# Attention with its adjacency term: where the term is added, and the order of the last iteration

## What is computed

```python
scale = DIM_HEAD ** (-0.5)
q, k, v = ...
dots = einsum('bhid,bhjd->bhij', q, k) * scale
m2 = mask[:, None, :, None] & mask[:, None, None, :]
dots = where(m2, dots, -big)
attn = softmax(dots, axis=-1) * 0.33
adj = where(m2, adj[:, None], 0.0)
dist = where(m2, adj[:, None], big)
attn = attn + 0.33 * adj + 0.33 * exp(-dist)
out = einsum('bhij,bhjd->bhid', attn, v)
out = out.reshape(B, N, 512) @ W_out + b_out
```

## Time and profile before

| | |
|---|---|
| median of 3 runs | 2669.83 us (2668.64 to 2670.15) |
| the profiled execution | 2667.08 us |
| its span, from first to last instruction | 2665.1 us |
| mean granted clock of TensorE | 0.999 |
| TensorE busy | 2590.1 us, 97% |
| VectorE busy | 1856.3 us, 70% |
| ScalarE busy | 893.6 us, 34% |
| GpSimd busy | 469.0 us, 18% |
| HBM traffic | 36 GB/s over the span |

### The profile page before, as it was taken

How to read it: one execution, slowest core, us unless ns; L and a number is a source line. 1 busy time by engine, 2 the same in 40 slices (tenths; PEclk the granted TensorE clock), 3 DMA queues, 4 the chain that set the end, 5 groups by cost and what they waited for, 6 DMA issues and landing times.

```text
span 2665.1 us, 74512 instructions
## 1 busy us (share of the span) xinstructions
PE 2590.1 (97%) x30297; PEld 2183.5 (82%) x30297; DVE 1856.3 (70%) x4168; ACT 893.6 (34%) x2796; POOL 469.0 (18%) x746
## 2 busy tenths in 40 slices
PE   7999999999999999999999999999999999999998
PEld 5788888887888888788888888888888888888887
DVE  5888888888888888866655665764665665566565
ACT  3222222222222222343432432433333243243333
POOL 1222222222222222210110111011011011101101
PEclk9999999999999999999999999999999999999999
DMA  3211111111111111311101101101110110110100
GB/s 129 83 39 39 39 40 39 39 39 39 39 39 39 39 39 39 115 32 35 36 15 31 35 19 29 35 19 32 35 31 16 35 35 15 31 35 19 29 20 17
DMA packets 128229, 100.87 MB, mean 38 GB/s; under 512 B 86676, under 2 KB 88744, under 8 KB 127912
## 3 DMA queue, kind: packets, MB, share of 16 engines
q1 hardware_dynamic: 125872, 95.18, 11.6%
q10 hardware_dynamic: 2040, 1.13, 0.1%
HBM read 62.68 MB, written 33.55 MB: 36 GB/s over the span
## 4 chain that ended last, share of the span: by engine, by line
PE 86%; DVE 7%; ACT 3%; issue 2%; POOL 2%; DMA 0%; ACTq 0%; DVEq 0%; POOLq 0%
PE ps L1317 23%; PE ps L631 18%; PE ps L1302 14%; PE ps L1320 11%; PE ps L634 9%; PE ps L623 4%; PE ps L1344 3%; PE ps L1382 1%; PE ps L1357 1%; PE ps L1389 1%; POOL sm L261 1%; DVE sm L480 1%; POOL sm L263 1%; DVE sm L478 1%; ACT Fp L351 1%
## 5 line engine op out<-in xcount | busy, mean ns | idle before, releaser
L1174 DVE TENSOR_TENSOR Tl<-ps,Th 128x256 fp32r<-128x256 f32 (+1 forms) x576 | 227.7, 446 | 88.9 <-ACT Th L1100 74.7
L987 POOL TENSOR_TENSOR Fp<-Fp,mhalf 128x1 f32<-128x1 f32 x128 | 78.6, 614 | 1175.2 <-DVE Fp L1181 1175.2
L631 PE MATMUL ps<-W1h,Th 128*128 128x512 f32 x512 | 205.9, 402 | 1.9 <-DVE Tl L453 1.8
L631 PE MATMUL ps<-W2h,Th 128*128 128x512 f32 x512 | 203.9, 398 | 3.1 <-DVE Tl L488 1.1
L631 PE MATMUL ps<-W1l,Th 128*128 128x512 f32 x512 | 200.8, 392 | 0.0
L631 PE MATMUL ps<-W2l,Th 128*128 128x512 f32 x512 | 199.9, 390 | 0.0
L1105 ACT ACTIVATE R<-R 128x512 f32<-128x512 f32 x128 | 80.9, 632 | 352.2 <-DVE R L1215 352.2
L1129 ACT ACTIVATE E<-E,Fp 128x64 f32<-128x64 f32 x512 | 170.8, 340 | 32.5 <-DVE Fp L1249 31.3
L261 POOL TENSOR_SCALAR sm<-sm 128x1 f32<-128x1 f32 x192 | 78.9, 411 | 557.8 <-DVE sm L482 298.9
L1241 DVE COPY QK<-ps 128x512 f32<-128x512 f32 x64 | 44.1, 689 | 166.7 <-PE ps L1302 166.7
L1302 PE MATMUL ps<-Th,Wh 128*128 128x256 f32 x512 | 147.7, 288 | 0.0
(11 more groups left out here) (208 smaller groups left out, 6657.2 us busy)
## 6 DMA issues: line engine op xcount, KB each, us to landing
X<-in_x SPq DMA_DIRECT2D x64, 256.0 KB, 6.3
x<-R SPq DMA_DIRECT2D x64, 256.0 KB, 2.4
X<-x SPq DMA_DIRECT2D x64, 256.0 KB, 2.7
out<-E SPq DMA_DIRECT2D x64, 256.0 KB, 2.1
AB<-in_adj SPq DMA_DIRECT2D x504, 8.0 KB, 1.7
NX<-in_adj SPq DMA_DIRECT2D x128, 32.0 KB, 2.2
E<-in_L_W1T SPq DMA_DIRECT2D x8, 256.0 KB, 6.8
E<-in_L_W SPq DMA_DIRECT2D x4, 512.0 KB, 5.1
```

The costliest lines, as they stand in the source:

```text
L631: pe.matmul(out, Th[:, c, j * P:(j + 1) * P], R(j), start=(j == 0 and R is Rh), stop=False)
L1174: return dve.tensor_tensor(lo, ps, hi.bitcast(F32), ALU.subtract)
```

## The change

Four things are changed.

1. The adjacency term is built from the turned adjacency `AT` instead of the separately loaded `A`. Per tile it is 128x64 (rows j of the graph, columns i), so for four tiles 128x256 where `Cm` was 128x512. The eight loads of `A` are gone; two loads of a mask row in another layout (`mrowT`) and one of a mask column are new. On POOL the masks are multiplied first (the new `MT` before `MM`), the bias `BS` is next, and then come `BT`, the sum and its masking, all of them now 128x256. The exponential on ACT and `BT` on POOL now wait for both turnings (at_ok), and the turning of the next group (at) waits for both of them.
2. sm no longer adds the term. After ta has turned the attention in PSUM, one VectorE instruction (L1272 of the changed kernel) reads all 128x512 of it, adds `CT` and writes `AA`. ScalarE's part of ta is gone. TensorE signals once behind all four transposes, and av waits for that one instruction.
3. `END` is a list of its own, and `TRANSITION` is another list. `ORDER` is as it was.
4. SP's loop over the iterations of the second half is written out instead of looping on the engine. The vectors gamma, beta and a are loaded at the start of the program into the tile `Fp`, which is not yet used there, instead of an own tile.

```diff
-        A, MM, BT = (per_graph(W) for W in (flat(first.NX), first.v_all[:, :], first.wa_all[:, :]))
-        Cm, BS = (per_graph(first.adjacent[:, k:k + 2, :, :].rearrange("p a c j -> p (a c j)")) for k in (0, 2))
+        MM, BS = (per_graph(W) for W in (first.v_all[:, :], first.adjacent[:, 2:4, :, :].rearrange("p a c j -> p (a c j)")))
+        MT, BT = (first.wa_all[:, k * CH * C:(k + 1) * CH * C].rearrange("p (c i) -> p c i", c=CH) for k in range(2))
+        CT = first.adjacent[:, 0, :, :]
...
+        END = order(
+            "sm.0 sm.1 qk.1 ta.0 ta.1 rs4.0 s.2 av.0 av.1 s.3 sm.2 wo.0 z4.0 wo.1 sm.3 ta.2 ta.3 rs4.1 x4.0 av.2 wo.2 z4.1 "
+            "bo.2 x4.1 rs4.2 bo.3 av.3 wo.3 rs4.3 z4.2 z4.3 x4.2 x4.3")
...
# POOL, step cm
-                pool.tensor_scalar(BT[:, :, :, :], A[:, :, :, :], LG, None, ALU.mult).then_inc(bt3, 1)
+                pool.tensor_tensor(MT[:, :, :], MT[:, :, :], mcf[:, 2, :].unsqueeze(2).to_broadcast([P, CH, C]), ALU.mult)
...
+                for p in range(2):
+                    pool.wait_ge(at_ok[p], n)
+                pool.tensor_scalar(BT[:, :, :], AT[:, :, :], LG, None, ALU.mult).then_inc(bt3, 1)
...
-                pool.tensor_tensor(Cm[:, :, :, :], Cm[:, :, :, :], BT[:, :, :, :], ALU.add).then_inc(cm2, 1)
+                pool.tensor_tensor(CT[:, :, :], CT[:, :, :], BT[:, :, :], ALU.add).then_inc(cm2, 1)
                 pool.wait_ge(cm2, n)
-                pool.tensor_tensor(Cm[:, :, :, :], Cm[:, :, :, :], MM[:, :, :, :], ALU.mult).then_inc(cm_ok, 1)
+                pool.tensor_tensor(CT[:, :, :], CT[:, :, :], MT[:, :, :], ALU.mult).then_inc(cm_ok, 1)
...
# ACT, step cm
+                        act.copy(MT[:, :, :], mrowT[:, :, :])
                         act.copy(MM[:, :, :, :], mrow[:, :, :, :]).then_inc(row_ok, 1)
-                        act.activation(Cm[:, :, :, :], A[:, :, :, :], ACT.Exp, bias=ln_ld[:, :], scale=-1.0).then_inc(exp_adj, 1)
+                        for p in range(2):
+                            act.wait_ge(at_ok[p], each[ahead])
+                        act.activation(CT[:, :, :], AT[:, :, :], ACT.Exp, bias=ln_ld[:, :], scale=-1.0).then_inc(exp_adj, 1)
...
-                    if step == "ta":
-                        act.wait_ge(ta_psA, n[c])
-                        act.copy(AV(c)[:, 0:2 * P], psA[c][:, 0:2 * P]).then_inc(ta_sbA, 1)
...
# DVE, step at
+                        if each[ahead] > 1:
+                            dve.wait_ge(exp_adj, each[ahead] - 1)
+                            dve.wait_ge(bt3, each[ahead] - 1)
...
# DVE, steps sm and ta
-                            .then_inc(soft_ok, 1)
-                        dve.wait_ge(soft_ok, 3 * n[c])
+                            .then_inc(attn_ok, 1)
+                    if step == "ta":
+                        dve.wait_ge(ta_ps, n[c])
                         dve.wait_ge(cm_ok, each[ahead])
-                        dve.tensor_tensor(E4(c), E4(c), over_heads(Cm, c), ALU.add).then_inc(attn_ok, 1)
-                    if step == "ta":
-                        dve.wait_ge(ta_psB, n[c])
-                        dve.tensor_copy(AV(c)[:, 2 * P:4 * P], psB[c][:, 0:2 * P]).then_inc(ta_sbB, 1)
+                        dve.tensor_tensor(AV(c).rearrange("p (x m i) -> p x m i", x=2, i=C), scores(c).rearrange("p x n (y i) -> p x (n y) i", y=2),
+                                          CT[:, c, :].unsqueeze(1).unsqueeze(1).to_broadcast([P, 2, 4, C]), ALU.add).then_inc(ta_sb, 1)
...
# PE, steps ta and av
-                        for x, ready in enumerate((ta_psA, ta_psB)):
+                        for x in range(2):
...
-                            mm.then_inc(ready, 1)
+                        mm.then_inc(ta_ps, 1)
...
-                        alone(ta_sbA, n[c])
-                        pe.wait_ge(ta_sbB, n[c])
+                        alone(ta_sb, n[c])
```

More of the change, by code:

```diff
@@ L856, in convolutions_and_attention @@
             "xp.2+ x3.3+ qk.0+ xp.3+ cm.0+ v.2+ v.3+ s.0+ bo.1+ s.1+")
-        START, END = [e for e in ORDER if e[2]], [e for e in ORDER if not e[2]]
+        END = order(
+            "sm.0 sm.1 qk.1 ta.0 ta.1 rs4.0 s.2 av.0 av.1 s.3 sm.2 wo.0 z4.0 wo.1 sm.3 ta.2 ta.3 rs4.1 x4.0 av.2 wo.2 z4.1 "
+            "bo.2 x4.1 rs4.2 bo.3 av.3 wo.3 rs4.3 z4.2 z4.3 x4.2 x4.3")
         def pair_counts(it, reg):
             return [[reg(it * 2 + (a * 2 + p + 1)) for p in range(2)] for a in (0, 1)]
-        MASK_LOADS = 2 * CH + 1 + 4
+        MASK_LOADS = 1 + 4 + 2 + 1
         TRANSITION = [(int(half), entry) for half, entry in ((e[0], order(e[2:])) for e in (
[8 rows of a table removed]
-            "2:s.1+").split())]
[7 rows of a table added]
+            "2:bo.0+ 2:xp.2+ 2:z3.3+ 2:g2.3+ 2:x3.3+ 2:qk.0+ 2:rs3.3+ 2:xp.3+ 2:v.2+ 2:bo.1+ 2:cm.0+ 2:v.3+ 2:s.0+ 2:s.1+").split())]
         block = ctx.enter_context(nc.Block())
@@ L890, in load_masks @@
             def load_masks(tile):
[L892 to L895, removed]
                 sp.dma_start(mrow[:, :, :, :], mask_rows[bass.ds(tile, CH)].rearrange("t (g j) -> (t g j)", g=2).partition_broadcast(P))\
@@ L901, in load_masks @@
                                      allow_slow_non_contiguous=True).then_inc(masks_in, 16)
+                for g in range(2):
+                    sp.dma_start(mrowT[g * C:(g + 1) * C, :, :], mask_halves[g, bass.ds(tile, CH), :].partition_broadcast(C))\
+                        .then_inc(masks_in, 16)
+                sp.dma_start(mcol[:, 2, :], mask_cols[:, bass.ds(tile, CH)], allow_slow_non_contiguous=True).then_inc(masks_in, 16)
             def load_qkv(k):
@@ L948, in store @@
                 sp.dma_start(out_rows[bass.ds(t0 + c, 1)].rearrange("a r d -> (a r) d"), Z[c % 2]).then_inc(out_stored[c % 2], 16)
-            with sp.Fori(0, iters - 1) as it:
-                t0 = sp.snap(it * CH)
+            for it in range(iters - 1):
+                t0 = it * CH
                 for p in range(2):
                     for c in (2 * p, 2 * p + 1):
-                        sp.wait_ge(t_ps[0], sp.snap(t0 + (c + 1)))
-                        sp.wait_ge(b3_ok, sp.snap(t0 + (c + 1)))
+                        sp.wait_ge(t_ps[0], t0 + (c + 1))
+                        sp.wait_ge(b3_ok, t0 + (c + 1))
                         load_x(c, t0 + (CH + c))
-                    sp.wait_ge(at_ok[p], sp.snap(it + 1))
+                    sp.wait_ge(at_ok[p], it + 1)
                     load_blocks(t0 + CH, p)
-                sp.wait_ge(cm_ok, sp.snap(it + 1))
+                sp.wait_ge(cm_ok, it + 1)
                 load_masks(t0 + CH)
@@ L1108, in steps @@
                         if each[ahead] > 1:
-                            act.wait_ge(attn_ok, (each[ahead] - 1) * CH)
+                            act.wait_ge(ta_sb, (each[ahead] - 1) * CH)
                         else:
```

23 lines of the change are left out of this document (13 added, 10 removed), and 15 rows, old and new, of the table TRANSITION.

## The result

| | before | after |
|---|---|---|
| median | 2668.89 us (5 runs, 2667.95 to 2670.15) | 2656.32 us (5 runs, 2654.58 to 2659.42) |
| ratio | | 0.9953, 95% interval 0.9939 to 0.9968 |
| profiled execution, span | 2667.08, 2665.1 | 2656.32, 2654.1 |
| mean granted clock | 0.999 | 0.999 |

Faster by 12.6 us where 7.6 were forecast, just outside the range. The sign and the end are as forecast, the hand-over has the wrong sign, and the loop gained almost three times its term.

A forecast was written before the change was run, and what follows sets the result against it. TensorE, busy 97%, was taken as the bound, so only its waits and clock pay. Loop -3.3, hand-over -0.3, end -2.4, clock -1.6 sum to -7.6 us: 2662.2 us from a median of 2669.83, range 2656.5 to 2668.5.

The forecast's parts named there:

- Place one: Before the first output projection wo.0 in each loop turn: VectorE's whole evictions make wo.0 0.14 us later.
- (c): Rival: slower, VectorE's eviction becomes the bound, +9 us in the loop less 2.4, 2676.4 us; chance 0.07.
- Places two and three: Before t0.0 and g0.0 in each turn: without the SBUF add g0.0 comes 0.22 us earlier, wo.0's delay included.
- The loop term: 15 turns of the attention loop, each 0.22 us shorter: -3.3 us.
- Everything at zero: ScalarE, GpSimd and the DMA queue: their changed work counted as zero, covered while TensorE works on projections.
- Hand-over: Between the halves, new list: y3.1 fills a 2.56 us wait, y3.2 loses cover; -0.3 us, between -1.5 and +1.
- The weight piece: In the hand-over's new list: a weight piece is moved ahead into a pause; part of the -0.3 us term.
- The end: Last iteration: wo.3 starts earlier, -2.4 us, and the clock stays up there, -1.6 us.
- The clock term: Last projection wo.3: the clock stays up instead of falling to half, -1.6 us, the less sure term; other end 0.
- (a): Rival: the gain stays at the end alone, the loop gives 0; 2665.8 to 2667.4 us; chance 0.31.
- (b): Rival: the loop gains but the clock falls all the same at the end; 2663.8 us; chance 0.14.
- (d): Rival: no wait follows g0.0's chain, -0.5 us a turn, -7.5 for the loop; 2658.0 us; chance 0.06.

The follow-up runs named there:

- b1: Changed kernel with the old TRANSITION, the old END and 32 spare bytes in front of Vh; 2663.41 us, ratio to before 0.9977.
- d3: Kernel before with 32 spare bytes in front of Vh, the new END and y3.1 alone moved ahead, without the moved term; 2663.56 us against 2670.27.
- a1: Kernel before with 32 unused bytes in front of the value weights Vh and Vl; 2666.35 us against 2670.21, ratio 0.9985.
- c3: Changed kernel with the old TRANSITION, in which only y3.1 is moved, in front of t3.2; its hand-over took 160.17 us.
- c4: Changed kernel with its new TRANSITION, in which only y3.1 is moved back behind t3.2; its hand-over took 161.71 us.
- a4: Changed kernel with the old END, the last iteration following the rest of ORDER; 2658.73 us.
- a2: Changed kernel with 32 spare bytes in front of Vh and Vl; 2660.99 us.
- c1: Changed kernel with the old TRANSITION, 32 spare bytes in front of Wh and 96 behind Wl; 2677.79 us against 2669.24 before.
- d1: Changed kernel with the old TRANSITION, y3.1 alone ahead of t3.2, 32 spare bytes in front of Wh and 224 behind Wl; 2652.50 us, ratio 0.9936.
- d2: c3 run again: changed kernel with the old TRANSITION and y3.1 alone in front of t3.2; 2655.98 us against 2670.27 before.
- a3: Changed kernel with the old TRANSITION; 2656.95 us against 2670.21 before.

## Why the prediction was wrong

It forecast a gain of 7.6 us; 12.6 were measured. Against its steps:

- **Place one**: +0.14 us at wo.0; measured +0.10. The step with two starts 0.61 apart holds (1.20 for two). The evicting add takes 0.69 us, as the sum assumed; by the Trainium skill's figures (VectorE: DVE Perf Modes, the section on the TRN2 errata) it would have been, as an estimate, 65 ns dearer, and the trace doesn't show that. Nor did the eviction by one engine become a bound, which was rival (c): VectorE's busy time fell from 1856 to 1829 us.
- **Places two and three**: g0.0 0.22 earlier with the 0.14 included; measured 0.30, and 0.32 (b1) and 0.34 (d3) a turn in the experiments. The chain was read right but 0.08 too long: t0.0 came 0.31 earlier, not 0.25, and from x4.0 to the remainder were 0.45 us, not 0.5. The chain then ended before TensorE did, so what bounds g0.0 now is av.2 behind its new wait of 0.25 us. The loop term should have been -4.5, not -3.3: under-sized, mechanism right.
- **Everything at zero**: the step that failed. The prediction counted engines and queues and has no term for where the tiles lie. The new mask tiles move Vh from 224 to 0 modulo 256 bytes against the features: 48 matmuls a turn by 5.8 ns, 0.28 us, 15 times, is -4.2. The trace before had a sign of it: around v.1 the eight matmuls of W2h stand 0.229 us apart, the twelve of the values 0.234. Without a run that moves the tile (a1) nothing said that the place was the reason.
- **Hand-over**: -0.3 forecast, +2.0 measured, beyond the bound of +1. y3.1 in front of the wait does no harm (c3), but its gain of 0.3 is not shown either. The weight piece "moved ahead into a pause" was mis-read: the pause is ScalarE's, but VectorE's part of the piece runs beside an operation of GpSimd for gs.3 and makes it 0.83 us longer, t2.3 waits 0.65 longer, and the rest of the list costs 1.35 us in all (c4). What of the last 0.4 is the turning's was not taken apart. The rest of the 2.0, some 0.6, is the clock, which fell in this profiled execution and not in that of before. It is no property of the new list: it fell in 3 of the 5 profiled executions with the old list, 4 of the 7 with the new one, and in none of the 4 with y3.1 alone ahead, which are too few to show a rule. The prediction had taken the clock into account only at the end.
- **The end**: -4.0 forecast, -4.0 measured. wo.2 came 8.88 us behind wo.0 (forecast 8.98), wo.3 13.61 (forecast 13.48), the clock stayed up. Of this 1.4 us need the term in the eviction (d3), which the prediction counted under the list. The clock term is no property of the old END: with it the clock fell in a4 and not in b1, which is worth 1.5 us.
- **The chances**: rivals (a) and (c) are out, and so is (b), since the clock stayed up before wo.3; (d), no wait behind g0.0's chain, is half true: no wait is left there, but it gives 0.30 a turn and not 0.5. Without the shifted weights (a2) the change measures 9.2 us, inside the range.

The sum as it should have stood: -4.5 - 4.2 + 2.0 - 4.0 = -10.7 of the 11.0 between the spans. The rest is +0.6 in the first half and -0.8 in the loop, where three turns of before were up to 0.5 us longer than the others. In two of them t0.0 waits 0.69 us instead of 0.34, in the third av stops for 0.36; why stays open.

## What to carry to other kernels

Adding a term in an eviction that must happen anyway is worth the removed operation only as far as a wait stands behind it: read the three or four waits that its queue feeds, and what comes next in each. A change that adds or drops a tile moves all that is allocated behind it: compare the start addresses of both operands of the hot matmuls, modulo 256 bytes, before and after. And a list with several moves should be tried one move at a time, and a pause looked for on every engine that the moved step uses: here one move did no harm, and the others together cost 1.35 us.

## What the runs showed of the hardware

- Matmuls of 128x512 in fp32r follow each other by 0.2275 us when the tiles of moving and stationary operand start 0 apart modulo 256 bytes (0.2299 for the values in c1), and by 0.2333 at 32, 160, 192 and 224, a little less at 128. In c1, where all six weights other than the values are away from 0, it was 21 us of 2656, the gain in the queries and keys included. What in the chip makes the distance count is not shown.
- With stationary weights and moving features of 256 columns the sign turns: 0.1208 us at distance 0, 0.1184 to 0.1188 at 32 (d1), 160, 192 and 224. A third of them read their stationary operand from Th and Tl themselves, where the low halves of these weights lie, so their distance never changes; from d2 to d1 they speed up like the others (119.8 and 120.0 ns to the next start become 117.8 and 118.3). So the distance of Wh and Wl goes with the pace of the whole stretch, not of their own matmuls alone. Why the sign turns stays open; only distances were varied, not the order in which operands are read.
- The granted clock in the hand-over fell to the level of 1.2 GHz behind a wait of 2.56 us in a1, a3 and b1, and not in before, with the same wait at the same place, nor in c1 with one of 2.5. Where TensorE waited 0.98 and 1.38 us instead (c3) it stayed at 2.4 GHz. Window of before and of a1, from t3.2 on (its length, PE, PEld, DVE, ACT, POOL busy; PEclk, DMA share, GB/s):

```profile
1103.00:1112.00 9.00, 8.60 (x127) 6.76 (x128) 8.51 (x22) 2.84 (x8) 2.38 (x6) 1.00 0.96 325
```

```profile
1104.60:1109.00 4.40, 4.40 (x45) 3.56 (x46) 4.18 (x11) 1.59 (x3) 1.17 (x4) 0.61 0.98 350
```

- In a1, a3 and b1 the hand-over took 1.15, 1.2 and 2.7 us more than in before; whether the clock falls there may be a part of the scatter of the medians, which no run here separates.
- GpSimd's operation on 128x1 (L263 before) takes some 0.57 us in nearly all of its 192 executions, and 1.40 us (c4) or 1.48 (before, at 1090.48) where it starts within 0.25 us behind the start of VectorE's subtraction of 128x1024 with both operands in SBUF (L1174, L1182). What the two share is not shown by these runs.
